# Forming dt·x·B of a state-space scan on TensorE from diagonal blocks, with the scan reading PSUM

## The reference, cut to what matters

```
x_dbl = x @ W_x                       # 64 columns for dt, 16 for B, 16 for C
dt    = softplus(x_dbl[:64] @ W_dt + b_dt)
A     = -exp(A_log)
h     = exp(dt * A) * h + (dt * x) * B_t        # scan over 512 time steps, h is [256, 16]
y     = sum over n of h * C_t
out   = residual + ((y + x * D) * silu(z)) @ W_out
```

## Time and profile before

| what | value |
|---|---|
| median of 3 runs (lowest, highest) | 1673.01 us (1671.74, 1675.35) |
| profiled execution, span of its instructions | 1673.0 us |
| busy share PE, PE weight loads, DVE, ACT, POOL | 78%, 48%, 67%, 41%, 29% |
| mean granted TensorE clock | 0.884 of full speed |
| state-space loops of the first pair (first n_db to the last scan) | 548.15 to 627.6 us, 659.81 to 737.3 us |

### The profile page before, as it was taken

How to read it: one execution, slowest core, us unless ns; L and a number is a source line. 1 busy time by engine, 2 the same in 40 slices (tenths; PEclk the granted TensorE clock), 3 DMA queues, 4 the chain that set the end, 5 groups by cost and what they waited for, 6 DMA issues and landing times.

```text
span 1673.0 us, 17199 instructions
## 1 busy us (share of the span) xinstructions
PE 1308.8 (78%) x5912; PEld 799.2 (48%) x5912; DVE 1126.0 (67%) x1997; ACT 685.1 (41%) x1136; POOL 493.3 (29%) x349
## 2 busy tenths in 40 slices
PE   0997768898977575669969967679988957747698
PEld 0675334576654122227636744336766622212366
DVE  5666655445775997987646665545556769889765
ACT  4443434343435344424425415253444443344244
POOL 2001000000644573646410010000016536547365
PEclk9998979899998677869979979799999977877899
DMA  5203030000000000000002020200000000000000
GB/s 204 57 14 88 4 89 3 1 1 1 1 1 0 1 0 0 1 1 1 13 33 70 19 71 22 70 3 1 1 1 1 1 0 1 0 1 0 1 1 19
DMA packets 23401, 33.11 MB, mean 20 GB/s; under 512 B 2992, under 2 KB 19152, under 8 KB 22864
## 3 DMA queue, kind: packets, MB, share of 16 engines
q1 hardware_dynamic: 23312, 31.99, 6.6%
HBM read 24.44 MB, written 8.06 MB: 19 GB/s over the span
## 4 chain that ended last, share of the span: by engine, by line
PE 47%; DVE 31%; issue 9%; DMA 5%; ACT 5%; POOL 1%; SPq 1%; POOLq 0%; DVEq 0%; ACTq 0%
PE bank L1227 10%; PE bank L1229 10%; PE bank L1228 10%; DVE n_h L1194 6%; DVE n_db L1186 4%; DVE a_mx L1132 3%; PE bank L1300 3%; PE bank L1236 2%; PE bank L1446 2%; DMA X<-in_x_dram 2%; PE bank L1486 2%; PE bank L1354 2%; DMA a_k<-stack_dram 2%; PE bank L1427 2%; DVE m_t L1057 1%
## 5 line engine op out<-in xcount | busy, mean ns | idle before, releaser
L590 POOL TENSOR_TENSOR m_hhl<-m_h,m_hhh 128x512 fp32r<-128x512 f32 x144 | 186.3, 1297 | 272.0 <-ACT m_hhh L755 271.7
L1536 PE MATMUL bank<-n_hc,ident 128*128 128x512 f32 x256 | 191.5, 861 | 83.1 <-POOL n_hc L623 79.8
L623 POOL TENSOR_TENSOR n_hc<-n_h,n_cs 128x512 f32<-128x512 f32 x128 | 210.4, 1662 | 128.9 <-DVE n_h L1194 123.7
L997 DVE SCALAR_TENSOR_TENSOR f_hl<-bank,f_hh 128x512 fp32r<-128x512 f32 x192 | 132.1, 690 | 128.1 <-ACT f_hh L695 127.0
L566 POOL TENSOR_TENSOR small<-small,half 128x4 f32<-128x4 f32 x24 | 24.3, 1012 | 600.3 <-DVE small L900 599.2
L695 ACT ACTIVATE f_hh<-bank 128x512 fp32r<-128x512 f32 x192 | 114.7, 597 | 207.1 <-PE bank L1300 206.7
L1194 DVE TENSOR_TENSOR_SCAN n_h<-n_da,n_db 128x512 f32<-128x512 f32 x128 | 192.0, 1538 | 3.4 <-POOL n_hc L623 2.3
L831 ACT ACTIVATE n_da<-n_dt,amat 128x512 f32<-128x512 f32 x128 | 91.7, 721 | 187.4 <-DVE n_h L1194 167.5
L1057 DVE TENSOR_TENSOR m_t<-m_sl,bank 128x512 f32<-128x512 f32 x128 | 87.8, 686 | 96.0 <-PE bank L1229 82.1
L1536 PEld LDWEIGHTS bank<-n_hc,ident 128*128 128x128 f32 x256 | 52.8, 241 | 187.0 <-POOL n_hc L623 177.1
L1132 DVE TENSOR_REDUCE a_mx<-bank 128x1 f32<-128x384 f32 (+3 forms) x176 | 105.9, 639 | 47.5 <-PE bank L1488 46.5
(11 more groups left out here) (247 smaller groups left out, 2820.4 us busy)
## 6 DMA issues: line engine op xcount, KB each, us to landing
w_stage<-in_mw_dram SPq DMA_DIRECT2D x16, 384.0 KB, 3.2
a_q<-stack_dram SPq DMA_DIRECT2D x8, 512.0 KB, 5.6
a_k<-stack_dram SPq DMA_DIRECT2D x16, 256.0 KB, 7.7
stage_fw<-in_fw_dram SPq DMA_DIRECT2D x2, 1536.0 KB, 10.0
stack_dram<-R SPq DMA_DIRECT2D x16, 192.0 KB, 2.8
stack_dram<-R SPq DMA_DIRECT2D x16, 128.0 KB, 2.5
stage_b<-in_bias_dram SPq DMA_DIRECT2D x1, 1728.0 KB, 10.2
X<-in_x_dram SPq DMA_DIRECT2D x5, 256.0 KB, 2.8
```

The costliest lines, as they stand in the source:

```text
L590: m_lo.by(nc.gpsimd.tensor_tensor(m_hh[1][:, i % 3, :], m_h[:, i % 3, :], m_hh[0][:, i % 3, :].bitcast(F32), ALU.subtract))
L623: n_hcs.by(nc.gpsimd.tensor_tensor(n_hc[:, m, :], n_h[:, m, :], n_cs[:, n // 2 % 2, :], ALU.mult))
L997: f_lo.by(V.scalar_tensor_tensor(f_h[1][:, i % 4, :], bank[:, i % 3, :], 0.0, f_h[0][:, i % 4, :].bitcast(F32), ALU.max, ALU.subtract))
L1536: n_ya.by(mm(bank[:, 2 + m, :], ident[:], n_hc[:, m, :], start=n == 2, stop=n == NSTATE + 1))
```

## The change

B is no longer spread over the partitions by a bf16 matmul and multiplied on DVE. PE forms dt·x·B itself: for each of four time tiles of 128 steps, the stationary operand is dt·x transposed (time on the partitions, 128 channels as columns), and the moving operand is a 128x128 diagonal matrix with the tile's 128 values of B on its diagonal. The result, channels by time, lies in PSUM (banks 0, 1 for even states, 4, 5 for odd ones), and the scan reads it there.

- The diagonal blocks: ACT copies the identity with a per-partition scale, 4 instructions of 128x128 per state, into two buffers (n_dg). For that it needs B with time on the partitions, n_bT, made once per unit by 8 small fp32 matmuls (16 columns each) and an ACT copy.
- The transposed dt·x: 8 fp32 transposes on PE once per unit into banks 2 and 3, and two ACT copies back into n_dtx.
- The rows of C: SP writes the 16 rows of C (x_dbl rows 80 to 95) to DRAM (32 KB) and reads each row back spread over 128 partitions (256 KB each), into a ring of three buffers (n_row). Row n waits for POOL's second product of state n-3.
- Removed: the two spreading matmuls per state, ACT's copy of the C row, DVE's n_db products, and the split into bf16 parts (ACT, DVE, POOL once per unit).

The diff, cut to its core:

```diff
                     if kind == "mamba":                      # SP
+                        sp.wait_ge(n_dtc.sem, n_dtc.at(k, 0))
+                        n_bcw.by(sp.dma_start(state_dram[p], n_xd[80:96]))
+                        sp.wait_ge(n_bcw.sem, n_bcw.at(k, 0))
+                        for n in range(NSTATE):
+                            if n >= ROWS:
+                                sp.wait_ge(n_hcs.sem, n_hcs.at(k, 2 * (n - ROWS) + 1))
+                            n_bcl[n % ROWS].by(sp.dma_start(
+                                n_row[:, n % ROWS], state_dram[p, n:n + 1].to_broadcast([P, T])))
...
                             pool.wait_ge(n_scan.sem, n_scan.at(k, n))        # POOL
-                            pool.wait_ge(n_csc.sem, n_csc.at(k, n // 2))
+                            row_in(pool, k, n // 2)
...
-                n_dtc.by(act.activation(n_dtr[:], bank[0:64, 4, :], ACT.Copy))     # ACT
-                n_bc1.by(act.activation(n_bc[64:96], bank[64:96, 4, :], ACT.Copy))
+                n_dtc.by(act.activation(n_xd[:], bank[0:96, 4, :], ACT.Copy))
...
+                act.wait_ge(n_bts.sem, n_bts.at(k, 0))
+                n_btc.by(act.activation(n_bT[:], bank[:, 5, 0:NT * NSTATE].rearrange("p (t n) -> p t n", t=NT), ACT.Copy))
                 act.wait_ge(n_dts.sem, n_dts.at(k, 0))
+                act.wait_ge(n_btc.sem, n_btc.at(k, 0))
                 for n in range(NSTATE):
+                    if n >= 2:
+                        act.wait_ge(n_dbs.sem, n_dbs.at(k, 2 * n - 3))
+                    for t in range(NT):
+                        ins = act.activation(n_dg[:, n % 2, t, :], ident[:], ACT.Copy, scale=n_bT[:, t, n:n + 1])
+                    n_dgs.by(ins)
+                    if n == 0:
+                        act.wait_ge(n_dxt.sem, n_dxt.at(k, 0))
+                        for m in range(NHALF):
+                            n_dxc.by(act.activation(n_dtx[:, m, :], bank[:, 2 + m, :], ACT.Copy))
                     for m in range(NHALF):
                         if n >= 1:
                             act.wait_ge(n_scan.sem, n_scan.at(k, 2 * n + m - 2))
                         n_das.by(act.activation(n_da[:, m, :], n_dt[:, m, :], ACT.Exp, scale=amat[:, m, n:n + 1]))
-                    act.wait_ge(n_cr.sem, n_cr.at(k, n))
-                    if n >= 2:
-                        act.wait_ge(n_hcs.sem, n_hcs.at(k, 2 * n - 3))
-                    n_csc.by(act.activation(n_cs[:, n % 2, :], bank[:, n % 2, :], ACT.Copy))
...
                 for n in range(NSTATE):                                       # DVE
-                    dve.wait_ge(n_br.sem, n_br.at(k, n))
-                    for m in range(NHALF):
-                        i = 2 * n + m
-                        if n >= 1:
-                            dve.wait_ge(n_scan.sem, n_scan.at(k, i - 2))
-                        n_dbs.by(V.tensor_tensor(n_db[:, m, :], n_dtx[:, m, :], bank[:, 4 + n % 2, :], ALU.mult))
...
-                        n_scan.by(V.tensor_tensor_scan(n_h[:, m, :], n_da[:, m, :], n_db[:, m, :], 0.0,
+                        n_scan.by(V.tensor_tensor_scan(n_h[:, m, :], n_da[:, m, :], bank[:, db_bank(n) + m, :], 0.0,
...
+                for t in range(NT):                                           # PE
+                    for m in range(2):
+                        ins = mm(bank[:, 5, t * NSTATE:(t + 1) * NSTATE], n_xc[:, m, t * P:(t + 1) * P], wx[:, m, 64:80],
+                                 start=m == 0, stop=m == 1)
+                n_bts.by(ins)
...
+                pe.wait_ge(n_dtxs.sem, n_dtxs.at(k, 0))
+                for m in range(2):
+                    ins = back(2 + m, n_dtx[:, m, :])
+                n_dxt.by(ins)
+                pe.wait_ge(n_dxc.sem, n_dxc.at(k, 1))
                 for n in range(NSTATE + 2):
                     if n < NSTATE:
-                        if n >= 2:
-                            pe.wait_ge(n_dbs.sem, n_dbs.at(k, 2 * n - 3))
-                        n_br.by(mm(bank[:, 4 + n % 2, :], pick[:, n:n + 1].to_broadcast([96, P]), n_bc[:],
-                                   start=True, stop=True))
-                        if n >= 2:
-                            pe.wait_ge(n_csc.sem, n_csc.at(k, n - 2))
-                        n_cr.by(mm(bank[:, n % 2, :], pick[:, 16 + n:17 + n].to_broadcast([96, P]), n_bc[:],
-                                   start=True, stop=True))
+                        pe.wait_ge(n_dgs.sem, n_dgs.at(k, n))
+                        for m in range(NHALF):
+                            if n >= 2:
+                                pe.wait_ge(n_scan.sem, n_scan.at(k, 2 * n + m - 4))
+                            for t in range(NT):
+                                ins = mm(bank[:, db_bank(n) + m, t * P:(t + 1) * P], n_dxT[:, m, t, :],
+                                         n_dg[:, n % 2, t, :], start=True, stop=True)
+                            n_dbs.by(ins)
```

More of the change, by code:

```diff
@@ L268, in program @@
         n_hc = sb("n_hc", [P, NHALF, T], F32, s)
[L269 to L272, removed]
+        n_row = sb("n_row", [P, ROWS, T], F32, s)
+        n_bT = sb("n_bT", [P, NT, NSTATE], F32, s)
+        n_dg = sb("n_dg", [P, 2, NT, P], F32, s)
         s.close()
         n_cv = n_cor = n_hc
-        n_abs, n_u, n_ln, n_low, n_pos = n_db, n_h, n_da, n_cs, n_dtx
+        n_abs, n_u, n_ln, n_pos = n_db, n_h, n_da, n_dtx
+        n_low = n_dg[:].rearrange("p a t d -> p a (t d)")
+        n_dxT = n_dtx[:].rearrange("p m (t d) -> p m t d", t=NT)
         stack_dram = nc.dram_tensor("stack_dram", [2, 2, P // 2, HEADS // 2, T], BF16, kind="Internal").ap()
         max_dram = nc.dram_tensor("max_dram", [QUADS, 12, T], BF16, kind="Internal").ap()
+        state_dram = nc.dram_tensor("state_dram", [2, NSTATE, T], F32, kind="Internal").ap()
         signals = []
@@ L395, in program @@
         n_dtc = sig("n_dtc", "mamba", 1)
[L396 to L399, removed]
+        n_bcw = sig("n_bcw", "mamba", 1, 16)
+        n_bcl = [sig(f"n_bcl_{r}", "mamba", len(range(r, NSTATE, ROWS)), 16) for r in range(ROWS)]
         n_dtp = sig("n_dtp", "mamba", 2)
@@ L408, in program @@
         n_dtxs = sig("n_dtxs", "mamba", 1)
-        n_br = sig("n_br", "mamba", NSTATE)
-        n_cr = sig("n_cr", "mamba", NSTATE)
         n_das = sig("n_das", "mamba", 2 * NSTATE)
-        n_csc = sig("n_csc", "mamba", NSTATE)
+        n_bts = sig("n_bts", "mamba", 1)
+        n_btc = sig("n_btc", "mamba", 1)
+        n_dxt = sig("n_dxt", "mamba", 1)
+        n_dxc = sig("n_dxc", "mamba", 2)
+        n_dgs = sig("n_dgs", "mamba", NSTATE)
         n_dbs = sig("n_dbs", "mamba", 2 * NSTATE)
@@ L439, in unit_end, with db_bank, row_in @@
                 eng.wait_ge(pair_done, j + 1)
+        def db_bank(n):
+            return 4 * (n % 2)
+        def row_in(eng, k, n):
+            eng.wait_ge(n_bcl[n % ROWS].sem, n_bcl[n % ROWS].at(k, n // ROWS))
         def job_bank(i):
@@ L619, in _ @@
                             pool.wait_ge(n_scan.sem, n_scan.at(k, n))
-                            pool.wait_ge(n_csc.sem, n_csc.at(k, n // 2))
+                            row_in(pool, k, n // 2)
                             if n >= 2:
                                 pool.wait_ge(n_ya.sem, n_ya.at(k, n - 2))
-                            n_hcs.by(nc.gpsimd.tensor_tensor(n_hc[:, m, :], n_h[:, m, :], n_cs[:, n // 2 % 2, :],
+                            n_hcs.by(nc.gpsimd.tensor_tensor(n_hc[:, m, :], n_h[:, m, :], n_row[:, n // 2 % ROWS],
                                                              ALU.mult))
```

29 lines of the change are left out of this document (9 added, 20 removed).

## The result

| | before | after |
|---|---|---|
| median (lowest to highest), us | 1673.49 (1671.74 to 1675.35) | 1683.74 (1682.47 to 1685.62) |
| executions | 4 | 4 |
| profiled execution: span, mean granted clock | 1673.0, 0.884 | 1681.8, 0.917 |

The ratio is 1.0065, with a 95% interval of 1.0047 to 1.0083: slower by about 11 us. The forecast was 1676 in a range of 1651 to 1708, with slower as the likeliest sign.

A forecast was written before the change was run, and what follows sets the result against it. Scans and POOL's products excluding each other set 4.49 us a state; afterwards a ring through ACT and PE. Terms gave +1.8 us per first unit, -0.1 per second, two of each +3.4 on 1673.0: 1676, range 1651 to 1708.

The forecast's parts named there:

- rival B: State-space loop: PE keeps falling to the half clock, 4.9 to 5.3 us a state, about 1710 us; chance 0.17.
- rival C: State-space loop: a scan with one PSUM operand still excludes POOL, +8 us a loop, about 1709 us; chance 0.06.
- Rival D: State-space loop: blocks at 0.4 us and slower hand-offs, 4.7 us a state, +5 a loop, 1696 us; chance 0.1.
- head: Before dt·x: eight small products ahead of the W_dt product delay its start, +0.8 us a unit.
- end: After the last scan: POOL's late product no longer delays DVE, -0.9 us in the first unit, nothing in the second.
- start: From dt·x to first scan: transposes, copies and first products at half clock take 5.3 us, +4.1 a unit.
- ring: State-space loop: closed wait path through ACT, PE, POOL, DVE, 8.75 us per two states, gaining 1.8 us a loop.
- insertions: Next unit's DVE steps inside the loop hide in DVE's idle time: -2.9 us first unit, -4.0 second.
- clock: State-space loop: granted clock similar to attention's 0.94, one short drop a loop, about +1.5 us.
- W_out product: After the second unit's loop: a busier PE speeds this product from 3.78 to 2.05 us, taken as -1.7 us.
- rival A: State-space loop: no ring, DVE really was the bound, insertions vanish wholly, about 1647 us; chance 0.2.
- C rows by DMA: POOL's C rows in the loop: loads land before they are needed, cost 0, bounds 0 and 1 us a state.

The follow-up runs named there:

- two traces of one kernel: Changed kernel with 14 unused products on PE ahead of dt·x, traced twice; medians 1682.1 and 1680.8 us.
- the half dose: Kernel before, with only the first half's n_db product written to PSUM and scanned there, the second half's left in SBUF; 1628.4 us.
- Two cuts and one lengthening: Changed kernel with next state's blocks ahead of the exps (1623.8 us), with two n_hc buffers per half (1615.2), and with block copies issued twice (1724.5).
- the two kernels without the ring: Changed kernel with state n+1's blocks ahead of state n's exps (1623.8 us), and changed kernel with two n_hc buffers per half (1615.2 us).
- the exps moved: Changed kernel with the next unit's four routing exps on ACT behind state 9's exps instead of state 8's; 1670.8 us, ratio 0.9999.

## Why the prediction was right, and where it was not

The time and the mechanism of the loop were right: 1676 forecast, 1683.7 measured, inside the likeliest case's own range of 1664 to 1688. The sign was right too, but in part by luck. The sum gave +3.4 us, hardly more than the 3.3 us that it gives as what can be told from no change, and most of the chance of slower stood on rivals B, C and D, of which none came true. The kernel is slower by 11 us because of a wait that the sum had not seen; with that wait moved away it is the same as before (0.9999). By its steps, from the scans' starts in the two traces (first of a pair of units, then second; the head is from ACT's first copy into n_xp to the end of dt·x, the end from the last scan's start to the first y step):

| step | forecast: first, second | first unit | second unit |
|---|---|---|---|
| head, n_xp to dt·x | +0.8, +0.8 | -0.1 | +0.7 |
| start | +4.1, +4.1 | +4.1 | +4.1 |
| first to last scan: cold states, ring, insertions, clock | -2.2, -3.3 | -2.4 | +2.1, +2.5 |
| end | -0.9, 0 | -0.9 | -1.2, -0.9 |
| W_out product | 0, -1.7 | 0 | 0 |
| sum | +1.8, -0.1 | +0.6 | +5.7, +6.4 |

The third row lumps four terms of the sum, so its -2.4 for -2.2 does not show that each of them was right. One was not: the ring gave 15 x 0.035 = 0.5 us a loop, where 1.8 was forecast, and the others made up for it. The -0.1 of the first unit's head is luck as well: from PE's first pass on n_xp to dt·x it takes 21.19 us before and 21.90 after in all four units, +0.7 as forecast, and the rest is that ACT's second copy into n_xp stood 1.22 us behind its first before and 0.63 after, which other runs of the changed head show either way. The end of the second unit moved by -1.2 and -0.9 for 0: DVE's first routing step behind the last scan took 1.42 us beside POOL's product before and 0.48 after.

Two of each come to +13.4. The spans differ by 8.8: the other 4.6 us lie in layers that neither kernel does differently, and two traces of one kernel (above) lay 13 us apart.

- **The port (rival C).** Right: no scan over 1.222 us, POOL's products at 1.27 (the longest, 1.45, starts at 743.43, beside DVE's routing step of 743.26 to 743.74). By the Trainium skill (GPSIMD Engine Reference, Key points) GpSimd contends with VectorE instructions that have two SBUF inputs; the trace agrees, and the half dose shows it operand by operand: with one operand in PSUM the scan beside POOL costs nothing, with two SBUF operands POOL's product takes up to 2.22 us instead of 1.26.
- **The ring.** Right in its links, 8.91 us a round for 8.75. By size: the exp 0.72 us for 0.63, the four blocks 1.18 for 1.14 + 0.09, the 16 products 2.05 for 1.79, the sum 0.88 for 0.86 + 0.17, the two scans 2.41 for 2.33. The hand-offs differ among themselves, 0.02 to 0.15 us, the longest through POOL's queue, and come to about 0.4 for 0.48. Two cuts and one lengthening, at other places each, answer to it. Rival D's slope is right too (four more copies made the round 1.16 us longer and the state 0.58), its size is not: a block follows the last in 0.292 us, near the 0.285 taken.
- **DVE as the bound (rival A).** Out in the changed kernel: DVE is busy 35.0 of 60 us. What A had right is what lies behind the ring: once it is cut, the states cost PE's 3.50 us. Its price was wrong: it kept the ring's gain of 1.8 us a loop, though states at 3.50 instead of 4.49 give 15 us, and the two kernels without the ring measured 1623.8 and 1615.2, not 1647.
- **The clock (rival B).** 0.94 from 568 to 628 us, as the +1.5 assumed; no run shows the +1.5 by itself. One fall that remains, at 705 us, comes in the 5.21 us in which PE waits for ACT.
- **The start.** 5.32 us for 5.3. But the half clock's share of it was mis-sized: the prediction took 1.9 us for it, it is 0.9, since the table load and the exps, at 548.08 with the fast clock, are nearly as late.
- **The step that failed: insertions in the second unit.** The prediction gave the second unit -4.0 us on the argument that a step on DVE hides in the time that DVE idles. That looks at the inserted work only on the engine that does it. One of these steps feeds ACT, and ACT waits for it in order, ahead of the blocks: 4.4 us idle, the ring empty, then a slow clock. The scans' part came out at +2.1 and +2.5 for -3.3: 5.4 to 5.8 us a unit, twice. With the exps moved, that part is -2.2 and -3.4 in the two second units, near the forecast's -3.3. The wait was in the trace of before, 5.35 us long and free of charge, since nothing behind it on ACT was needed sooner.
- **The W_out product** of the second unit still takes 3.78 us, where -1.7 had been forecast: 5.4 us of routing on DVE stand between the last scan's end and the first y step (743.34 to 748.71), in which PE has little to do, and it idles 3.28 us right ahead of the product. Timeline of PE after:

```profile
751.61 3.78 PE L1555 MATMUL bank<-wout,n_db 128*128 128x128 f32 x16 [3.28 <-DVE n_db L1209]
```

- **C rows by DMA.** Right: 3.1 us to landing, and no row names a DMA as what POOL waited for.

Why does a change that frees 1.07 us a state bring nothing? Because it gave the freed time away to a ring of its own making: a state costs 3.42 us with DVE's products left where they were, and 4.455 us with PE's.

## What to carry to other kernels

A two-SBUF-input scan on DVE beside elementwise work on POOL is worth one operand in PSUM, by itself and first: here 3.6% by where one result is written. When a product moves to another engine, write down the closed path through all in-order queues (what stands ahead of what on each) and sum it once around; where it exceeds each engine's own work, issue the producer one step earlier or add one buffer. And look through the before-trace for waits that cost nothing today (here 5.35 us on ACT): each is a charge for whatever the change puts behind it.

## What the runs showed of the hardware that was not expected

- In these rows the exclusion falls on whichever comes second, and only on it: in the half dose 64 scans with two SBUF operands never took over 1.227 us while POOL's products beside them took up to 2.22; in the kernel before scans reached 2.230.

```profile
L1194 DVE TENSOR_TENSOR_SCAN n_h<-n_da,n_db x64: 1191/1224/1227, 547.9 to 1512.2; 128x512 f32<-128x512 f32 x64
```

- A DVE product written to PSUM costs the same as one written to SBUF: two in 1.27 us where the earlier trace rows have 1.25 and 1.29.
- ACT copies of 128 columns with a scale column take 0.386 us each but follow each other every 0.292 us; eight in a row keep that pace.
- Keeping PE at the full clock by unused products makes the stage behind it faster in the trace (transposes 1.97 to 1.09 us, and the granted clock in that stretch below) and does not show in the times, which scatter by 9 and 11.5 us over 7 and 10 executions. Where it ran too long it cost its own gain again (5.2 us for 4.4).

```profile
546.00:550.00 4.00, 2.05 (x16) 1.86 (x16) 1.10 (x1) 3.97 (x8) 0.00 (x0) 1.00 0.00 0
```
